# Cross-attention on one Trainium2 core: smaller pieces and another order of work in the value phase

## The reference

```python
Q = (img_embed @ Wq).reshape(B, -1, H, D).transpose(0, 2, 1, 3)
K = (sent_embed @ Wk).reshape(B, -1, H, D).transpose(0, 2, 1, 3)
V = (sent_embed @ Wv).reshape(B, -1, H, D).transpose(0, 2, 1, 3)
score = jnp.einsum('bhqd,bhkd->bhqk', Q, K) / math.sqrt(D)
attn = jax.nn.softmax(jnp.where(mask, score, -jnp.inf), axis=-1)
out = einsum('bhqk,bhkd->bqhd', attn, V).reshape(B, -1, H * D) @ Wo + img_embed
return layernorm(out) * gamma + beta
```

## Time and profile before

| | us |
|---|---|
| median of 3 runs | 369.8 (369.56 to 370.49) |
| the profiled execution | 369.25 |
| its span, first to last instruction | 367.4 |

### The profile page before, as it was taken

How to read it: one execution, slowest core, us unless ns; L and a number is a source line. 1 busy time by engine, 2 the same in 40 slices (tenths; PEclk the granted TensorE clock), 3 DMA queues, 4 the chain that set the end, 5 groups by cost and what they waited for, 6 DMA issues and landing times. The chain is left out here.

```text
span 367.4 us, 7130 instructions
## 1 busy us (share of the span) xinstructions
PE 345.0 (94%) x2328; PEld 311.6 (85%) x2328; DVE 290.9 (79%) x555; ACT 243.7 (66%) x794; POOL 237.1 (65%) x234
## 2 busy tenths in 40 slices
PE   8999999997599983999999999999999999999994
PEld 6999999885478773999899899898889889889884
DVE  2169997696967752689889889889889889889896
ACT  2277655654447716888778778777787787787461
POOL 2046440984639963857886886885976976976233
PEclk9999999999899997999999999999999999999999
DMA  7998679757533006104404404404314314313003
GB/s 245 428 416 318 227 289 331 280 205 267 195 121 122 10 8 238 52 1 173 142 31 171 143 32 171 139 35 174 104 70 171 122 52 171 115 59 115 30 30 114
DMA packets 21348, 56.25 MB, mean 153 GB/s; under 512 B 2560, under 2 KB 4928, under 8 KB 19392
## 3 DMA queue, kind: packets, MB, share of 16 engines
q1 hardware_dynamic: 20448, 54.81, 41.5%
q10 hardware_dynamic: 864, 1.00, 0.8%
HBM read 46.98 MB, written 8.39 MB: 151 GB/s over the span
## 5 line engine op out<-in xcount | busy, mean ns | idle before, releaser
L794 PE MATMUL pair<-vw_hi,pt_hi 128*128 128x512 f32 x155 | 62.1, 401 | 0.0
L794 PE MATMUL pair<-vw_hi,pt_lo 128*128 128x512 f32 x155 | 60.9, 393 | 0.0
L794 PE MATMUL pair<-vw_lo,pt_hi 128*128 128x512 f32 x155 | 60.7, 392 | 0.0
L1489 POOL TENSOR_TENSOR out_sb<-centred,beta_sb 128x512 f32<-128x512 f32 x30 | 38.8, 1292 | 29.0 <-ACT centred L1010 29.0
L719 PE MATMUL pair<-a_hi,xo_hi 128*128 128x304 f32 x128 | 40.3, 315 | 7.5 <-ACT pair L942 7.5
L1534 POOL TENSOR_TENSOR xo_lo<-x_sum,xo_hi 128x512 fp32r<-128x512 f32 x32 | 41.3, 1295 | 7.4 <-ACT xo_hi L989 7.4
L965 ACT ACTIVATE prob<-c,neg_max 128x77 f32<-128x77 f32 x128 | 43.9, 346 | 0.0
L719 PE MATMUL pair<-a_lo,xo_hi 128*128 128x304 f32 x128 | 39.0, 304 | 0.0
L719 PE MATMUL pair<-a_hi,xo_lo 128*128 128x304 f32 x128 | 38.8, 303 | 0.0
L1003 ACT ACTIVATE pt_hi<-pair 128x640 fp32r<-128x640 f32 x32 | 22.5, 703 | 23.5 <-PE pair L781 23.5
L1321 DVE TENSOR_TENSOR pair<-pair,x_in 128x512 f32<-128x512 f32 x31 | 21.7, 699 | 18.6 <-PE pair L794 17.0
(11 more groups left out here) (140 smaller groups left out, 1069.2 us busy)
## 6 DMA issues: line engine op xcount, KB each, us to landing
w_out<-wo SPq DMA_DIRECT2D x8, 1024.0 KB, 6.0
xt_in<-x_tiles SPq DMA_DIRECT2D x16, 512.0 KB, 3.9
x_in<-x_rows SPq DMA_DIRECT2D x16, 512.0 KB, 4.8
out<-out_sb SPq DMA_DIRECT2D x31, 256.0 KB, 2.2
w_out<-wq_t SPq DMA_DIRECT2D x7, 1024.0 KB, 7.8
w_proj<-wv SPq DMA_DIRECT2D x8, 768.0 KB, 5.0
w_proj<-wk SPq DMA_DIRECT2D x6, 768.0 KB, 9.5
w_out<-wq_t SPq DMA_DIRECT2D x2, 512.0 KB, 7.8
```

The costliest lines, as they stand in the source:

```text
L794: mm = pe.matmul(ps_out[:, i % 2, 0:s.model], ps[:, j, :], v[:, j, b, :], start=(j == 0 and n == 0), stop=(j == s.key_t - 1 and n == len(p ...
L1489: pool.tensor_tensor(out_sb[i % OUT_RING][:, :], centred[i % 2][:, :], beta_sb[:, :], ALU.add)\
```

## The change

1. `RESTS`: GpSimd's lo of `w_out` is taken in four pieces of 512 columns, not two of 1024; TensorE waits piece by piece. VectorE's own (the last head's) now comes ahead of `split_kv(15)`.
2. The sums and splits of the right operands are spread over u = 8 to 14 (seven heads) on VectorE, and their roundings over u = 8 to 13 on ScalarE. The three `t_sb` buffers swap roles so that heads 6 and 7 need less of them free. The bias rows and one clearing of padding move to u = 13, the other to u = 14.
3. `take_strips` copies the 26 rows of each strip side by side (four copies of 26 x 128 for one of 128 x 128). A head then needs two row DMAs of 13 rows x 512 columns, 16 in all for 64.
4. In the last head the main product comes first and the strips last. `round_blocks(0)` moves one iteration earlier, ahead of `split_vw(5)`.
5. After the value phase only the remainder rows of batch 0 are split; batch 1's follow after `split_pt(1)` on ScalarE and `split_pt(2)` on VectorE. `out_rows` and `centre(0)` wait accordingly, and `combine_c12(0)` waits for head 6's row DMAs, since `strip_sb` now lies over `c12`.

```diff
@@ placement, order of completions, t_sb
+            strip_sb = [early.enter_context(nc.sbuf_tensor(f"strip_sb{n}", [P, s.model], F32)) for n in range(2)]
 def main_done(h):
-            return 2 * (H + h) + (1 if h < H - 1 else 2)
+            return 2 * (H + h) + 1
 def strips_done(h):
-            return 2 * (H + h) + (2 if h < H - 1 else 1)
+            return 2 * (H + h) + 2
 def right_steps(b):
-            x, y, z, w = t_sb[b][:, :, :], t_sb[s.batches][:, :, :], sum_z, sum_w
+            x, y, z, w = t_sb[2 * b][:, :, :], t_sb[1][:, :, :], sum_z, sum_w
@@ sync: move_strips
-                for g in range(STRIPS):
-                    for n in range(s.batches):
-                        b = (h + n) % 2
-                        to, at = place(h, b) * s.rest, g * STRIP + n * s.rest
-                        sp.dma_start(rest_rows[to:to + s.rest, b, g * P:(g + 1) * P],
-                                     strip_sb[h % 2][at:at + s.rest, :]).then_inc(ld_rest[h % 2], DMA_INC)
+                for n in range(s.batches):
+                    b = (h + n) % 2
+                    to = place(h, b) * s.rest
+                    sp.dma_start(rest_rows[to:to + s.rest, b, :], strip_sb[h % 2][n * s.rest:(n + 1) * s.rest, :])\
+                      .then_inc(ld_rest[h % 2], DMA_INC)
@@ tensor: value_product, out_rows, loop
-                        pe.wait_ge(dve_o_lo if by_vector(u) else pool_o_lo,
-                                   rests_before(u, by_vector(u)) + k // 2 + 1)
+                    if not by_vector(u):
+                        pe.wait_ge(pool_o_lo, 2 * rests_before(u, False) + k + 1)
+                    elif k % 2 == 0:
+                        pe.wait_ge(dve_o_lo, rests_before(u, True) + k // 2 + 1)
...
+                if i % s.per_batch == 0:
+                    pe.wait_ge(dve_vw_lo, 2 * H + b + 1)
...
-                elif u < USES - 1:
+                else:
+                    if u == USES - 1:
+                        open_bank_a()
                     value_product(u)
                     value_strips(u)
-                else:
-                    open_bank_a()
-                    value_strips(u)
-                    value_product(u)
@@ scalar: split_vw, take_strips, loop
                 elif h // 2 == FREE_VW:
-                    act.wait_ge(dve_t_lo, len(T_PARTS))
+                    act.wait_ge(dve_t_lo, t_no[T4, 0])
+                    act.wait_ge(dve_t, t_done(T2, 1))
...
-                act.activation(strip_sb[h % 2][:, :], ps_strips, ACT.Copy).then_inc(act_strip, 1)
+                for g in range(STRIPS):
+                    e = act.activation(strip_sb[h % 2][0:s.rest_toks, g * P:(g + 1) * P],
+                                       ps_strips[g * STRIP:g * STRIP + s.rest_toks, :], ACT.Copy)
+                e.then_inc(act_strip, 1)
...
+                if u == H + 1:
+                    round_t(T3, 0)
+                elif u == H + 4:
+                    round_t(T3, 1)
+                elif u == USES - 3:
+                    round_blocks(0)
+                elif u == USES - 2:
+                    round_sums(0)
+                elif u == USES - 1:
+                    seed(0)
                     round_blocks(1)
-                    split_vw(u - H)
+                split_vw(u - H)
+                take_strips(u - H)
+                if u == H:
+                    round_t(T1, 0)
+                elif u == H + 1:
+                    round_t(T2, 0)
+                elif u == H + 2:
+                    round_t(T4, 0)
+                elif u == H + 3:
+                    round_t(T1, 1)
+                elif u == H + 4:
+                    round_t(T2, 1)
+                elif u == H + 5:
+                    round_t(T4, 1)
             copy_s1(0)
-            split_rest()
+            split_rest(0)
...
             split_pt(1)
+            split_rest(1)
             exps_second(1)
@@ vector: loop
+                if H <= u < USES - 1 and by_vector(u + 1):
+                    split_w_out(u + 1)
                 if u + 1 < USES and not whole_out(u + 1):
                     split_kv(u + 1)
...
+                if u == H:
+                    right_sum(0, 0, 3)
+                elif u == H + 1:
+                    right_sum(0, 5, 6)
+                    split_t(T1, 0)
+                    split_t(T3, 0)
+                elif u == H + 2:
+                    split_t(T2, 0)
+                    right_sum(0, 6, 8)
+                elif u == H + 3:
+                    split_t(T4, 0)
+                    right_sum(1, 2, 4)
+                elif u == H + 4:
+                    right_sum(1, 5, 6)
+                    split_t(T1, 1)
+                elif u == H + 5:
+                    split_t(T2, 1)
+                    right_sum(1, 6, 8)
+                elif u == H + 6:
                     split_t(T4, 1)
...
                 split_vw(u - H)
...
+                if u == H:
+                    right_sum(0, 3, 5)
+                elif u == H + 2:
+                    right_sum(1, 0, 2)
+                elif u == H + 3:
+                    right_sum(1, 4, 5)
                 elif u == H + 4:
+                    split_t(T3, 1)
+                elif u == H + 5:
+                    clear_pad(vw_lo)
                     bias_rows()
-                elif u == H + 5:
+                elif u == H + 6:
                     clear_pad(vw_hi)
-                    clear_pad(vw_lo)
...
-            for b in range(s.batches):
-                split_rest(b)
+            split_rest(0)
@@ gpsimd
-                    for half in range(2):
-                        pool.wait_ge(act_o_hi, 2 * split_before(u) + half + 1)
-                        pool.tensor_tensor(half_cols(values_lo(u), half), half_cols(w_out_sb[u % W_RING], half),
-                                           half_cols(w_out_hi[u % 2], half).bitcast(F32), ALU.subtract)\
+                    for k in range(s.dim_t):
+                        if k % 2 == 0:
+                            pool.wait_ge(act_o_hi, 2 * split_before(u) + k // 2 + 1)
+                        pool.tensor_tensor(values_lo(u)[:, k, :, :], w_out_sb[u % W_RING][:, k, :, :],
+                                           w_out_hi[u % 2][:, k, :, :].bitcast(F32), ALU.subtract)\
                             .then_inc(pool_o_lo, 1)
```

More of the change, by code:

```diff
@@ L182, in build @@
         t_hi, t_lo = [t_hi0, t_hi1], [t_lo0, t_lo1]
+        with ExitStack() as early:
+            strip_sb = [early.enter_context(nc.sbuf_tensor(f"strip_sb{n}", [P, s.model], F32)) for n in range(2)]
         c12 = sb("c12", [P, s.half])
-        with ExitStack() as early:
-            strip_sb = [early.enter_context(nc.sbuf_tensor(f"strip_sb{n}", [P, P], F32)) for n in range(2)]
         prob_rest = [sb(f"prob_rest{n}", [P, s.rest_rows]) for n in range(2)]
@@ L923, in take_strips, with split_rest @@
                 if h >= 2:
-                    act.wait_ge(ld_rest[h % 2], DMA_INC * STRIPS * s.batches * (h // 2))
-                act.activation(strip_sb[h % 2][:, :], ps_strips, ACT.Copy).then_inc(act_strip, 1)
-            def split_rest():
-                for n in range(2):
-                    act.wait_ge(ld_rest[n], DMA_INC * STRIPS * s.batches * (H // 2))
-                act.wait_ge(dve_pad, 2)
-                for b in range(s.batches):
-                    act.activation(vw_hi[0:s.rest_rows, s.key_t - 1, b, :], rest_rows[0:s.rest_rows, b, :], ACT.Copy)\
-                       .then_inc(act_vw_hi, 1)
+                    act.wait_ge(ld_rest[h % 2], DMA_INC * s.batches * (h // 2))
+                for g in range(STRIPS):
+                    e = act.activation(strip_sb[h % 2][0:s.rest_toks, g * P:(g + 1) * P],
+                                       ps_strips[g * STRIP:g * STRIP + s.rest_toks, :], ACT.Copy)
+                e.then_inc(act_strip, 1)
+            def split_rest(b):
+                if b == 0:
+                    for n in range(2):
+                        act.wait_ge(ld_rest[n], DMA_INC * s.batches * (H // 2))
+                    act.wait_ge(dve_pad, 2)
+                act.activation(vw_hi[0:s.rest_rows, s.key_t - 1, b, :], rest_rows[0:s.rest_rows, b, :], ACT.Copy)\
+                   .then_inc(act_vw_hi, 1)
             def seed(p):
@@ L1034, in _ @@
                     round_w_proj(u + 2)
-                if H < u <= H + 4:
-                    b = (u - H - 1) // 2
-                    if (u - H) % 2:
-                        round_t(T3, b)
-                        round_t(T2, b)
-                if u == USES - 2:
-                    round_blocks(0)
-                    round_sums(0)
                 if u < H:
@@ L1198, in bias_rows, with right_sum @@
                        .then_inc(dve_rows, 1)
-            def right_sum(n, b):
-                if n == T1:
-                    dve.wait_ge(dve_a_lo, 2 * H)
-                if n == T1 and b > 0:
-                    dve.wait_ge(dve_t_lo, t_no[T2, b - 1])
-                elif n == T4:
-                    dve.wait_ge(dve_t_lo, t_no[T2, b])
```

(17 more changed lines are left out.)

34 lines of the change are left out of this document (6 added, 28 removed).

## The result

The changed kernel takes 355.8 us (median; 353.96 to 357.78) against 369.7 for the kernel before it in the same rounds: a ratio of 0.9624, interval 0.9568 to 0.9679, or 3.8% faster. The forecast was 356.2, in a range of 353 to 361. The profiled execution took 355.5 us, with a span of 353.7, against 369.25 and 367.4.

The account below looks back on a forecast made before the run. TensorE was taken as the row phase's bound, its waits before that as the gain: 5.5 (value phase) + 6.0 (restart) + 1.8 (clock) = 13.3 us off 369.25 gives 355.95, by the median 356.2; range 353 to 361.

Parts of the forecast that it names:

- The bound: Row phase: TensorE busy 192.5 of 197 us, work the change doesn't shrink, so the gain must come from before it.
- (e): From the end of the value phase (T) to TensorE's restart at T+7.6: stall 1.5 us for 7.5, gain 6.0.
- (c): ScalarE's strips: four copies make 1.1 us for 0.28, covered by its idle time except in the last head.
- (d): Row DMAs on SyncE's queue: two a head, 1.7 us, at 0.84 each despite rows of 2 KB for 512 bytes.
- the rival of slow row DMAs: Bigger row DMAs start and land slower, restart at T+10.2, lower clock returns: 360.6 us; chance 0.07.
- (b): VectorE's new list in the value phase, walked head by head: phase ends at 124.9, not 130.39; gain 5.5 us.
- (a): GpSimd's four pieces: +0.4 us a head, but a blocked VectorE instruction waits at most 1.29 us, not 2.4.
- The rival in which VectorE bounds the value phase: VectorE's and GpSimd's lists fill the heads, so the value phase gains only 2 us: 360 us; chance 0.18.
- slower-than-before one: GpSimd's pieces don't let VectorE in; a loss once the mean wait passes 1.6 us, 383 at 2.6; chance 0.03.
- The lower clock in the last head: Last main product, after a TensorE gap of 3.2 us: the lower clock was charged at 1.5 us.
- no lower clock: Last head: its gap doesn't bring the lower clock, 1.5 us less: 354.7 us, or 353; chance 0.2.
- (f): Moved work, such as batch 1's remainder split after the restart: no cost with 0.7 us of room, otherwise 0.5 lost.

Follow-up runs that it names:

- after: The changed kernel itself, against the kernel before it: 355.8 us, ratio 0.9624; run again as the yardstick, 356.1 us.
- halves: The changed kernel with GpSimd's two pieces of 1024 columns put back in place of four of 512: 356.2 us.
- earlier bias rows: The changed kernel with the two bias rows and one clearing moved to earlier heads in VectorE's list: 355.1 us.
- gap filled: The changed kernel with ten extra matmuls of 512 columns in TensorE's gap ahead of the last main product: 355.1 us.

## Why the prediction was right, point by point

**The bound: right.** The row phase beyond the first tiles did not change, and the whole gain came from ahead of it.

**(e), T to restart: right.** The chain, walked step by step: strips taken at T + 1.4 (122.88 + 1.11), DMAs through SyncE's queue at T + 3.0, forecast 3.1, landed T + 4.4, forecast 4.2, restart T + 7.8, forecast 7.6. TensorE waited 1.6 us, forecast 1.5, and the clock behind it stayed at 1.00. Two runs of their own bear out the part of the DMAs: 5.7 us back with 64 of them, 7.7 us gained by 16 alone.

**(c), (d): right, and cheaper.** A single line each from after, the row DMAs and the strip copies (ns min/median/max, first and last start):

```profile
L545 SPq DMA_DIRECT2D rest_rows<-strip_sb x16: 743/749/924, 72.8 to 124.8; - x16
L927 ACT ACTIVATE strip_sb<-pair x32: 266/268/273, 71.7 to 123.7; 26x128 f32<-26x128 f32 x32
```

A row of 2 KB starts as fast as one of 512 bytes; the rival of slow row DMAs is out. Four copies took 1.11 us, as forecast.

**(b), the value phase: mis-sized by 1.9 us.** The walk gave 57.1 us from the first main product to T, and 55.2 were measured. Its one early gap, 1.0 us at head 2, is absent, because `split_vw(1)` ended at 81.42, 0.2 us ahead of its deadline of 81.63. I had charged both lock waits of head 1 in full and the step is narrow: with GpSimd's halves the gap is there again, at 1.2 us. The last gap was 2.7 for 3.2 (the walk had the bank opening go ahead of it at once, and the opening itself waited 1.7 of the 2.7 for T4's lo) and the last product 5.3 for 5.5, and the rest, 0.2, is in heads of 7.14 us for 7.2.

**(a), GpSimd's pieces: the mechanism right, the weight somewhat smaller.** The prediction gave the lock 2 us of the value phase; the halves cost 1.2 us at one head in the trace, and the medians don't show it, since the executions with halves happened to have the higher clock. The rival in which VectorE bounds the value phase is out, as no head but the last waits for it, and so is the slower-than-before one: VectorE's six two-input instructions in the rows above took 8.2 / 6 = 1.37 us in the mean, 0.6 more than the 0.79 undisturbed, where that rival decides from 1.6 on.

**The lower clock in the last head: right in place and size (1.3 us for 1.5), and not in every execution.** Its rival, no lower clock, seems to have happened too: two of the nine executions of this program have a mean clock of 0.999 and 1.000 and end near 354 us. No trace was taken of those.

**(f), "moved at no cost": wrong.** This is the step that failed. The prediction counted the 1.8 us of the clock after the restart in full, and gave batch 1's remainder split 0.7 us of room. It named ScalarE's `exps_second(1)` behind it but not what stands behind it on VectorE, `centre(0)` and then the combination of the third pair, which TensorE's next products wait for. The price was 1.6 us, not the 0.5 at which the loss of cover was put. Moving it into idle slots brought it back. The prediction's own sign for this step, more than 221.6 us from restart to end, came true: 223.3.

**Part 4: priced only in part.** The prediction saw that "with the main product leading no strips fill the gap" and charged the clock for it, but never compared the two orders. The difference is 2.9 us: 1.4 for the clock, 1.0 for the strips in the gap and 1.6 for the wait at the restart, since the strips are also the head of the chain to it, less what the row phase takes back.

So that the forecast came within 0.4 us is partly luck. It rests on two misses of 1.9 and 1.7 us that cancel, and on 0.5 us from ahead of the first main product, which no step had claimed. I don't know where these 0.5 come from; in the second trace of the same kernel the first main product starts at 68.32, later than before, and over all traces here, with the same work ahead of it, at 67.35 to 68.59, so it may be scatter.

## What to carry to other kernels

When many small DMAs go through one queue ahead of a deadline, count their start time, not their bytes: 16 starts of 2 KB rows in place of 64 of 512 bytes, at the same 0.75 us each, were worth 7.7 us. Of the last items ahead of a change of phase, put first the one whose result has the longest chain behind it, and let the other fill the wait: the reverse order cost 2.9 us, 1.4 of them through the clock behind the longer gap. Work that is pushed behind a deadline is not free because it is late: ask on each in-order engine what stands behind it, and put it where that engine waits anyway (1.6 us here).

## What the runs showed of the hardware

VectorE's two-input instructions and GpSimd's block each other in both directions, and two streams of short instructions alternate: GpSimd's additions of 0.75 us took 1.72 beside VectorE's split of 128x1024, which itself went from 2.35 to 3.38 for the two halves. The Trainium skill, SBUF — State Buffer, describes a lock on the port pair that the two share, for either side ("the other fully blocks"), and the trace agrees. What I had not expected is that it can undo an edit: 2.8 us of work taken out of VectorE's list moved the next two-input instruction into GpSimd's stretch, and 1.0 of them were gone by the lock alone.

The clock after the same gap of some 2.7 us fell in both traces of the changed kernel, and by their mean clocks (0.999 and 1.000) not in two other executions. It stayed up in the traces with gaps of 2.4 us (halves) and 1.9 us (earlier bias rows). In a trace the lower clock costs 1.3 to 1.5 us there; the nine executions spread by more, from 353.96 to 357.78, and what makes the rest is not shown. With the gap filled they lay between 353.95 and 355.87, at 0.997 or more.
